# Causal attention on one NeuronCore: the four-block tile of each head takes its remainder through a PSUM bank

## The chip, the cores and the metric

The kernel runs on one core of one Trainium2 chip. The metric is the device time of one execution in microseconds. Engines are called PE (TensorE), ACT (ScalarE), DVE (VectorE), POOL (GpSimd) and SP (SyncE, which here only issues DMAs).

## The reference, cut to what matters

The whole program is one decoder layer on x of shape (4, 1024, 512): causal self attention with a linear position bias, cross attention against a context with a mask, and a quantised feed forward, each followed by a layer norm. The change touches the self attention alone:

```
q, k, v = heads(x @ Wq + bq), heads(x @ Wk + bk), heads(x @ Wv + bv)   # 16 heads of 32
scores = einsum('bhqd,bhkd->bhqk', q, k) / sqrt(32) + bias[None]
attn = softmax(scores, axis=-1)
out = einsum('bhqk,bhkd->bhqd', attn, v)
```

The bias is `slope * (k - q)` where allowed and -1e9 elsewhere. Even heads may look back (k <= q), odd heads forward (k >= q). There are 4 x 16 = 64 head instances of 1024 x 1024 scores, of which a little over half count.

## The kernel before

`attention_phase` is one function for both attentions; with `causal=True` it names its tiles `self_...`, without it `cross_...`. It holds one program for each engine, and the programs run loosely against each other through counting semaphores. Every engine carries out its own list strictly in order, so an instruction that waits holds up all that is behind it on that engine.

Work is cut into units `u`, 8 to a head and 32 to a loop pass (four heads, `HB`); `steps` runs first a prologue and then, for each step `t`, one call of `step(i, t, last)` on each engine. A head is worked twice over:

- **Row maxima** (`scores` L893 on PE, `maxima` L1128 on DVE). PE multiplies one block of 128 queries by all allowed keys into a score tile `sc[u % 2]` (two buffers). DVE adds the bias and takes the maximum of each row (L1147), which frees the buffer through the semaphore `taken`. Blocks come in the order big, small, big, small: widths 1024, 128, 896, 256, 768, 384, 640, 512. PE is 19 steps ahead with this (`SLEAD`).
- **Turning the maxima** (`turn_max` L907 on PE, `max_row` on ACT): once in a head the maxima are transposed through one of the `stp` banks and sent back by DMA as an extra row of the queries, so that the maximum is subtracted inside the next product.
- **Transposed scores** (`key_scores` L921 on PE, `exps` L1021 on ACT), 6 steps ahead (`ELEAD`). PE multiplies one block of 128 keys by all allowed queries (L939, with the triangle of the diagonal block added by L942), in chunks of at most 512 columns, into the two banks `stp[0]` and `stp[1]` in turn. ACT takes the exponential of each chunk in float32 into `p32` (L1033) and counts it in `expd`. PE may write chunk number c when chunk c-2 has been counted.
- **The remainder** (`low`, POOL L1239). The probability is used as two 16-bit parts: the upper half of the float32 word, read in place as bfloat16, and the remainder, p minus that upper half, which POOL writes as float16 into `plo`. In the self attention POOL does this for all eight tiles of a head; in the cross attention DVE does one in eight (L1161).
- **Values** (`values` L948 on PE). For each block of 128 queries PE adds upper part times values (L968) and remainder times values (L969) into the two output banks `ob`. It waits for `expd` and for POOL's count `lo_g`. The first tile of a head also waits for `o_read`, which says that the output banks of the head before have been read.
- **Finishing a head**: ACT copies half of the output banks (`oraw`, L1088), DVE adds the other half (`gather`, L1170, raising `o_read`), and two steps later DVE takes the reciprocal and writes the scaled result (`scale`, L1176 and L1183).

The order of a step on PE is: row scores of unit t+19, the turned maxima, transposed scores of unit t+6, values of unit t. On DVE it is: gather (when unit t is the first of a head), maxima of unit t+19, a remainder where DVE has one, scale. On ACT it is: exponentials of unit t+6, and the copies after the last unit of a head. Within a head the key blocks are taken in the widths 1024, 128, 896, 256, 768, 384, 640, 512, so the eighth unit of each head is the four-block tile of 512 columns: one chunk. Tiles of more than 512 columns are two chunks, so a head has 12 chunks. `p32` and `plo` hold eight units each. The PSUM banks are all in use: 4 for `sc`, 2 for `stp`, 2 for `ob`.

Row scores of an even numbered unit are at least 640 columns wide and use `sc[0]`; those of an odd numbered unit are at most 512 wide and use `sc[1]`.

Of the kernel before, what the change touches and what calls it, by code (L numbers as in the profile page):

```python
# [17 lines left out]
BF16 = mybir.dt.bfloat16  # L18
# [9 lines left out]
P = 128  # L28
# [543 lines left out]
def attention_phase(nc, c, name, causal, q_dram, k_dram, v_dram, out_dram, mb_dram=None, nm_dram=None, place_dram=None, kept=None, spare=None):  # L572
# [13 lines left out]
    with ExitStack() as ctx:  # L586
# [16 lines left out]
        osum = [sb(f"osum{j}", [P, ST, HD], F32) for j in range(2)]  # L603
        rden = [sb(f"rden{j}", [P, ST], F32) for j in range(2)]
        ost = sb("ost", [P, ST, HB * HD], F32)
        sc = [kit.ps(f"{name}_sc{j}", [P, S]) for j in range(2)]
        stp = [kit.ps(f"{name}_st{j}", [P, GT]) for j in range(2)]
        ob = [kit.ps(f"{name}_o{j}", [P, ST // 2, VW]) for j in range(2)]

# [5 lines left out]
        chunked = sem("chunked")  # L615
        expd = sem("expd")
        lo_v, lo_g = sem("lo_v"), sem("lo_g")
        pv_done = sem("pv_done")
        o_read = sem("o_read")
        o_recip, o_half, o_scaled = sem("o_recip"), sem("o_half"), sem("o_scaled")  # L620
# [85 lines left out]

        def on_vector(u):

            return not causal and u % UH == 4

        def width(u):

# [8 lines left out]
        def high_of(u):  # L721

            j, b = spot(u)
            return p32[j][:, b:b + width(u)].bitcast(BF16).rearrange("p (q h) -> p q h", h=2)[:, :, 1]

        def lows_of(u):
# [20 lines left out]
        with nc.Block() as block:  # L747
# [138 lines left out]
            @block.tensor  # L886
            def _(pe):
                def scores(i, u):

                    n, at, qt = rows_of(u)  # L890
                    j, slot = n % NQK, u
                    if at == 0:
                        pe.wait_ge(qk_in[j], (i + n // NQK + 1) * QKS)  # L893
                    pe.wait_ge(taken, i * (HB * UH) + slot + 1)
                    if not causal:
                        nc.tensor.matmul(sc[slot % 2][:, 0:GT], qa[j][0:HD, qt * P:(qt + 1) * P], ka[j][0:HD, 0:GT], start=True, stop=True)  # L896
                        nc.tensor.matmul(sc[slot % 2][:, GT:S], qa[j][HD:2 * HD, qt * P:(qt + 1) * P], kx[j][HD:2 * HD, :],  # L897
                                         start=True, stop=True).then_inc(scored, 1)
                        return
                    k0, k1 = key_range(n, qt)  # L900
                    for k in range(k0, k1, GT):
                        w = min(GT, k1 - k)
                        mm = nc.tensor.matmul(sc[slot % 2][:, k - k0:k - k0 + w], qa[j][0:3 * HD, qt * P:(qt + 1) * P],  # L903
                                              ka[j][0:3 * HD, k:k + w], start=True, stop=True)
                    mm.then_inc(scored, 1)

                def turn_max(i, n, cc, last=False):  # L907

                    pe.wait_ge(taken, i * (HB * UH) + (min(n + 1, HB) if last else n + 1) * UH + 2)
                    pe.wait_ge(expd, i * CS + cc + 1)  # L910
                    nc.tensor.transpose(stp[cc % 2][0:ST, 0:P], qmax[n % 2][:], c["idf"][:]).then_inc(chunked, 1)

                def ahead(i, u, last):
                    if within(last, u):
                        scores(i, u)

                def late_max(i, u, last):
                    if u % UH == TURN and within(last, u):
                        turn_max(i, u // UH + 1, turn_before(u), last)

                def key_scores(i, u):  # L921

                    n, at, kt = keys_of(u)
                    j = n % NQK
                    if at == 0:
                        pe.wait_ge(mrow_in[j], (i + n // NQK + 1) * 16)
                        if causal:
                            pe.wait_ge(place_in[j], (i + n // NQK + 1) * 16)
                    if at == 0 and isinstance(i, int) and i == 0:
                        pe.wait_ge(ready if n < 2 else ready_late, n % 2 + 1)  # L930
                    if not causal and n % HB == 0:
                        pe.wait_ge(nm_in[kt], (i + n // HB) // (H // HB) * 16 + 16)
                    cc = chunks_before(u)
                    for q0, q1 in chunks(n, kt):
                        pe.wait_ge(expd, i * CS + cc + 1)
                        w, out = q1 - q0, stp[cc % 2]
                        lhs = ka[j][0:KR, kt * P:(kt + 1) * P]
                        diag = causal and q0 <= kt * P < q1
                        mm = nc.tensor.matmul(out[:, 0:w], lhs, qa[j][0:KR, q0:q1], start=True, stop=causal)  # L939
                        if diag:  # L940
                            d = kt * P - q0
                            mm = nc.tensor.matmul(out[:, d:d + P], c["idbig"][:], tri[n % 2][:], start=False, stop=True, skip_group_check=True)  # L942
                        if not causal:
                            mm = nc.tensor.matmul(out[:, 0:w], c["idbig"][:], nm[kt][:, q0:q1], start=False, stop=True)  # L944
                        mm.then_inc(chunked, 1)
                        cc += 1

                def values(i, u):  # L948

                    n, at, kt = keys_of(u)  # L950
                    if at == 0:
                        pe.wait_ge(v_in[n % NQK], i * 16 + 16)
                        pe.wait_ge(o_read, (i * HB + n) * 2 + 2)
                    pe.wait_ge(expd, i * CS + chunks_by(u) + 2)
                    if on_vector(u):
                        pe.wait_ge(lo_v, i * LV + lows_by(u, True))
                    else:
                        pe.wait_ge(lo_g, i * LG + lows_by(u, False))
                    a, z = query_range(n, kt)
                    j, b = spot(u)  # L960
                    high, rest = high_of(u), plo[j][:, b:b + width(u)]
                    for qt in range(a // P, z // P):
                        q = slice(qt * P - a, qt * P - a + P)
                        out = ob[qt // 4]
                        first = at == 0 and qt % 4 == 0
                        last_kt = at == max(keys_of(n * UH + k)[1] for k in range(UH)
                                            if query_range(n, keys_of(n * UH + k)[2])[0] <= qt * P < query_range(n, keys_of(n * UH + k)[2])[1])
                        nc.tensor.matmul(out[:, qt % 4, :], high[:, q], vh[n % NQK][:, kt, :], start=first, stop=False, skip_group_check=True)  # L968
                        mm = nc.tensor.matmul(out[:, qt % 4, 0:HD + 1], rest[:, q], vh[n % NQK][:, kt, 0:HD + 1],  # L969
                                              start=False, stop=last_kt, skip_group_check=True)  # L970
                    mm.then_inc(pv_done, 1)
                    return mm

                def prologue():
                    for u in range(SLEAD):
                        ahead(0, u, False)
                        if u == UH + 1:
                            turn_max(0, 0, 0)
                        k = u - (SLEAD - ELEAD)
                        if k == 0 and causal:  # L980
                            pe.wait_ge(tri_made, 2)
                        if k >= 0:
                            late_max(0, k, False)
                            key_scores(0, k)

                def step(i, t, last):
                    ahead(i, t + SLEAD, last)
                    late_max(i, t + ELEAD, last)
                    if within(last, t + ELEAD):
                        key_scores(i, t + ELEAD)  # L990
                    values(i, t)

                steps(pe, prologue, step)
# [3 lines left out]
            def _(act):  # L997
# [23 lines left out]
                def exps(i, u):  # L1021
# [8 lines left out]
                    for q0, q1 in chunks(n, kt):  # L1030
                        act.wait_ge(chunked, i * CS + cc + 1)
                        bias = strip[n % NQK][:, S + kt:S + kt + 1] if causal else 0.0
                        nc.scalar.activation(p32[j][:, b + q0 - a:b + q1 - a], stp[cc % 2][:, 0:q1 - q0], ACT.Exp,  # L1033
                                             bias=bias, scale=SM).then_inc(expd, 1)
                        cc += 1
# [62 lines left out]
            def _(dve):  # L1098
# [55 lines left out]
                def low(i, u):  # L1154
                    n, at, kt = keys_of(u)
                    if not on_vector(u):
                        return
                    dve.wait_ge(expd, i * CS + chunks_by(u) + 2)
                    j, b = spot(u)
                    q = slice(b, b + width(u))  # L1160
                    nc.vector.tensor_tensor(plo[j][:, q], p32[j][:, q], high_of(u), ALU.subtract).then_inc(lo_v, 1)  # L1161

                def gather(i, n):

# [1068 lines left out]
```

## Time and profile before

| | |
|---|---|
| median of 3 runs | 3087.35 us (3085.69 to 3087.98) |
| profiled execution | 3089.86 us |
| its span, first to last instruction | 3088.1 us |
| mean granted TensorE clock | 0.936 |
| busy: PE, DVE, ACT, POOL | 85%, 73%, 61%, 59% |

The profile shows one execution. The self attention lies between about 370 and 975 us of its span, the cross attention between about 1138 and 2065 us. "Busy" is the time in which an engine had an instruction running; "idle before" is the gap in front of an instruction, with what ended it. PE's matmuls overlap, so their ends are modelled. On ACT, DVE and POOL the records of neighbouring instructions overlap slightly as well: by about 0.1 us on ACT and DVE and 0.04 us on POOL.

### The profile page before, as it was taken

To read this page: it belongs to the slowest core of one execution; us is meant where nothing else is said; L and a number is where in the kernel's file an instruction comes from. 1 tells how busy PE (TensorE), PEld (TensorE's weight loads), DVE (VectorE), ACT (ScalarE), POOL (GpSimd) and SP (SyncE) were. 2 spreads that over 40 slices of the span, in tenths; PEclk is the share of its full clock that TensorE was granted. 3 is DMA by queue.
4 is the path that set the end of the run, shared out by engine and by line. 5 is a ranking of instruction groups with operands and counts; after the bars stand their busy time and mean duration, and the time that the engine had idled before them with its cause. 6 is when DMAs were issued, how large, how long until landed. Compare 5 with 4: busy or idle time off the path is not lost. (4 is left out here: it accounts for less than half of the span.)

```text
span 3088.1 us, 77009 instructions
## 1 busy us (share of the span) xinstructions
PE 2625.1 (85%) x24103; PEld 1413.4 (46%) x24103; DVE 2253.0 (73%) x4459; ACT 1879.7 (61%) x3779; POOL 1808.1 (59%) x1209
## 2 busy tenths in 40 slices
PE   7999688888886869999999999962999899603999
PEld 4555245555554535555555555531444344301444
DVE  8888667777774777888888887847334477697776
ACT  3444377777775537777777777764333577695333
POOL 3444489999996319999999999986000244300000
PEclk9999789999998979999999999985999999856999
DMA  8999634444445661232131132135444688796332
GB/s 308 336 332 325 210 95 137 125 136 133 134 128 185 232 218 33 58 98 55 45 103 52 48 100 54 46 97 182 172 165 164 207 272 286 263 417 260 124 114 82
DMA packets 320616, 504.41 MB, mean 163 GB/s; under 512 B 36641, under 2 KB 158369, under 8 KB 320498
## 3 DMA queue, kind: packets, MB, share of 16 engines
q1 hardware_dynamic: 317026, 496.27, 48.3%
q0 software_dynamic: 1952, 6.29, 0.6%
q8 instruction: 55, 0.90, 0.1%
q10 hardware_dynamic: 1520, 0.43, 0.1%
q14 instruction: 63, 0.52, 0.1%
HBM read 266.10 MB, written 194.28 MB: 149 GB/s over the span
## 5 line engine op out<-in xcount | busy, mean ns | idle before, releaser
L1239 POOL TENSOR_TENSOR cross_plo<-cross_p 128x2048 f16<-128x2048 f32 (+1 forms) x256 | 850.4, 3350 | 77.2 <-ACT cross_p L1033 77.2
L1147 DVE CUSTOM_DVE_ANT_0 cross_junk<-cross_sc,rows 128x1024 bf16<-128x1024 f32 x512 | 622.7, 1223 | 149.3 <-PE cross_sc L897 146.3
L1033 ACT ACTIVATE cross_p<-cross_st 128x512 f32<-128x512 f32 x1024 | 556.3, 595 | 206.8 <-PE cross_st L944 206.8
L1239 POOL TENSOR_TENSOR self_plo<-self_p 128x1024 f16<-128x1024 f32 (+7 forms) x512 | 576.9, 1161 | 17.3 <-ACT self_p L1033 16.8
L1033 ACT ACTIVATE self_p<-self_st,self_strip 128x512 f32<-128x512 f32 (+3 forms) x768 | 415.6, 582 | 142.7 <-PE self_st L942 112.1
L1147 DVE CUSTOM_DVE_ANT_0 self_junk<-self_sc,self_strip 128x1024 bf16<-128x1024 f32 (+7 forms) x512 | 371.3, 752 | 135.2 <-PE self_sc L903 135.0
L939 PE MATMUL cross_st<-cross_qa,cross_ka 97*128 97x512 f16 x1024 | 396.0, 387 | 1.8 <-ACT cross_p L1033 0.7
L944 PE MATMUL cross_st<-rows,idbig 128*128 128x512 f16 x1024 | 391.6, 382 | 0.0
L968 PEld LDWEIGHTS cross_o<-cross_vh,cross_p 128*128 128x128 bf16 x4096 | 270.2, 97 | 76.2 <-issue 21.8
L968 PE MATMUL cross_o<-cross_vh,cross_p 128*128 128x65 f16 x4096 | 297.6, 191 | 4.9 <-POOL cross_plo L1239 4.5
L1851 POOL TENSOR_SCALAR v_w<-v_w 128x512 f32<-128x512 f32 x96 | 59.4, 618 | 401.9 <-ACT v_w L1828 401.9
L969 PE MATMUL cross_o<-cross_vh,cross_plo 128*128 128x33 f16 x4096 | 291.2, 179 | 0.0
L939 PE MATMUL self_st<-self_qa,self_ka 98*128 98x512 f16 (+3 forms) x768 | 246.7, 337 | 48.8 <-ACT self_p L1033 44.6
L969 PEld LDWEIGHTS cross_o<-cross_vh,cross_plo 128*128 128x128 f16 x4096 | 249.3, 96 | 53.4
L903 PE MATMUL self_sc<-self_ka,self_qa 96*128 96x512 f16 (+3 forms) x768 | 214.4, 336 | 34.0 <-DMA self_ka<-scr_k_hi 18.7
L968 PE MATMUL self_o<-self_vh,self_p 128*128 128x65 f16 x2304 | 200.1, 192 | 39.7 <-DVE self_osum L1170 19.8
L130 PE MATMUL gt_acc<-rows,wg_hi 128*128 128x512 f16 x768 | 230.5, 382 | 1.5 <-DVE rows L124 1.5
L896 PE MATMUL cross_sc<-cross_ka,cross_qa 32*128 32x512 f16 x512 | 200.6, 392 | 18.4 <-DMA cross_kx<-scr_k_hi 11.7
L897 PE MATMUL cross_sc<-cross_kx,cross_qa 32*128 32x512 f16 x512 | 200.6, 392 | 0.0
L968 PEld LDWEIGHTS self_o<-self_vh,self_p 128*128 128x128 bf16 x2304 | 164.0, 98 | 74.5 <-issue 44.2
L969 PE MATMUL self_o<-self_vh,self_plo 128*128 128x33 f16 x2304 | 192.5, 179 | 0.0
L939 PEld LDWEIGHTS cross_st<-cross_qa,cross_ka 97*128 97x128 f16 x1024 | 99.8, 97 | 187.8 <-ACT cross_p L1033 94.8
(263 smaller groups left out, 5845.6 us busy)
## 6 DMA issues: line engine op xcount, KB each, us to landing
self_strip<-self_strips SPq DMA_DIRECT2D x64, 516.0 KB, 3.2
scr_gate<-gt_y SPq DMA_DIRECT2D x96, 256.0 KB, 2.1
v_w<-scr_gate SPq DMA_DIRECT2D x96, 256.0 KB, 4.0
scr_h<-v_w SPq DMA_DIRECT2D x96, 256.0 KB, 4.1
j_h<-scr_h SPq DMA_DIRECT2D x48, 512.0 KB, 9.5
d_o<-scr_o SPq DMA_DIRECT2D x9, 1536.0 KB
scr_up<-v_y SPq DMA_DIRECT2D x48, 256.0 KB, 4.2
j_u<-scr_up SPq DMA_DIRECT2D x24, 512.0 KB, 12.1
```

What stands on the lines that cost most here:

```text
L130: mm = nc.tensor.matmul(out, a, b, start=(n == 0), stop=(n == len(terms) - 1))
L896: nc.tensor.matmul(sc[slot % 2][:, 0:GT], qa[j][0:HD, qt * P:(qt + 1) * P], ka[j][0:HD, 0:GT], start=True, stop=True)
L897: nc.tensor.matmul(sc[slot % 2][:, GT:S], qa[j][HD:2 * HD, qt * P:(qt + 1) * P], kx[j][HD:2 * HD, :], start=True, stop=True).then_inc(scor ...
L903: mm = nc.tensor.matmul(sc[slot % 2][:, k - k0:k - k0 + w], qa[j][0:3 * HD, qt * P:(qt + 1) * P], ka[j][0:3 * HD, k:k + w], start=True, st ...
L939: mm = nc.tensor.matmul(out[:, 0:w], lhs, qa[j][0:KR, q0:q1], start=True, stop=causal)
L944: mm = nc.tensor.matmul(out[:, 0:w], c["idbig"][:], nm[kt][:, q0:q1], start=False, stop=True)
L968: nc.tensor.matmul(out[:, qt % 4, :], high[:, q], vh[n % NQK][:, kt, :], start=first, stop=False, skip_group_check=True)
L969: mm = nc.tensor.matmul(out[:, qt % 4, 0:HD + 1], rest[:, q], vh[n % NQK][:, kt, 0:HD + 1], start=False, stop=last_kt, skip_group_check=True)
L1033: nc.scalar.activation(p32[j][:, b + q0 - a:b + q1 - a], stp[cc % 2][:, 0:q1 - q0], ACT.Exp, bias=bias, scale=SM).then_inc(expd, 1)
L1147: nc.vector.tensor_tensor_reduce(junk[slot % 2][:, 0:w], sc[slot % 2][:, 0:w], bias, 1.0, -3e38, ALU.add, ALU.max, qmax[n % 2][:, qt:qt + ...
L1239: nc.gpsimd.tensor_tensor(plo[j][:, a:z], p32[j][:, a:z], high, ALU.subtract).then_inc(lo_g, 1)
L1851: nc.gpsimd.tensor_scalar(wk[n % NW][:], wk[n % NW][:], 65536.0, MAGIC, ALU.mult, ALU.add).then_inc(inc, 1)
```

## The change

The four-block tile of each causal head, the eighth unit, is taken off POOL:

- `sc[1]` shrinks from two banks to one, and the bank that comes free becomes `whole`.
- PE writes the tile's transposed scores to `whole` instead of `stp[cc % 2]`. It first waits until DVE has finished with `whole` for the head before (`lo_v`).
- ACT takes the exponential twice: once rounded to bfloat16 into `p32` (semaphore `high_made`), once in float32 from `whole` back into `whole`; only the second counts in `expd`.
- DVE subtracts the bfloat16 values from `whole` and writes `plo`, in the step in which it does the maxima of the unit with 512 columns, after these. `values` waits for `high_made`, `expd` and `lo_v`.
- POOL has seven tiles left in a head. All other tiles, and the cross attention, are as they were.

```
-        sc = [kit.ps(f"{name}_sc{j}", [P, S]) for j in range(2)]
+        sc = [kit.ps(f"{name}_sc{j}", [P, GT if causal and j else S]) for j in range(2)]
...
+        if causal:
+            whole, high_made = kit.ps(f"{name}_whole", [P, GT]), sem("high_made")
...
         def on_vector(u):
 
-            return not causal and u % UH == 4
+            return u % UH == (UH - 1 if causal else 4)
...
         def high_of(u):
 
             j, b = spot(u)
+            if causal and on_vector(u):
+                return p32[j][:, b:b + width(u) // 2].bitcast(BF16)
             return p32[j][:, b:b + width(u)].bitcast(BF16).rearrange("p (q h) -> p q h", h=2)[:, :, 1]
...
                     cc = chunks_before(u)
+                    if causal and on_vector(u) and (not isinstance(i, int) or i > 0 or u >= UH):
+                        pe.wait_ge(lo_v, i * LV + lows_by(u, True) - 1)
                     for q0, q1 in chunks(n, kt):
                         pe.wait_ge(expd, i * CS + cc + 1)
-                        w, out = q1 - q0, stp[cc % 2]
+                        w, out = q1 - q0, whole if causal and on_vector(u) else stp[cc % 2]
...
                     pe.wait_ge(expd, i * CS + chunks_by(u) + 2)
+                    if causal and on_vector(u):
+                        pe.wait_ge(high_made, i * LV + lows_by(u, True))
...
                         bias = strip[n % NQK][:, S + kt:S + kt + 1] if causal else 0.0
+                        if causal and on_vector(u):
+                            nc.scalar.activation(high_of(u), whole[:], ACT.Exp, bias=bias, scale=SM).then_inc(high_made, 1)
+                            nc.scalar.activation(whole[:], whole[:], ACT.Exp, bias=bias, scale=SM).then_inc(expd, 1)
+                            continue
...
+                    if causal:
+                        dve.wait_ge(high_made, i * LV + lows_by(u, True))
                     dve.wait_ge(expd, i * CS + chunks_by(u) + 2)
...
-                    nc.vector.tensor_tensor(plo[j][:, q], p32[j][:, q], high_of(u), ALU.subtract).then_inc(lo_v, 1)
+                    nc.vector.tensor_tensor(plo[j][:, q], whole[:] if causal else p32[j][:, q], high_of(u), ALU.subtract).then_inc(lo_v, 1)
```

## Rows read from the trace of the kernel before

**Rows 1.** The page: span, and POOL's busy tenths in 40 slices of 77 us.

```profile
span 3088.1 us, 77009 instructions
...
POOL 3444489999996319999999999986000244300000
```

**Rows 2.** One stretch: busy us of PE, PEld, DVE, ACT, POOL; clock, DMA.

```profile
440.00:680.00 240.00, 202.14 (x2809) 127.63 (x2809) 183.49 (x535) 183.19 (x400) 239.58 (x213) 1.00 0.43 133
```

**Rows 3.** The line L1239 between 440 and 960 us, and who waited for it.

```profile
L1239 POOL TENSOR_TENSOR self_plo<-self_p x462: 392/1144/2077, 439.9 to 959.7; 128x512 f16<-128x512 f32 x20, 128x896 f16<-128x896 f32 x20, 128x384 f16<-128x384 f32 x19, 128x1024 f16<-128x1024 f32 x19
...
who waited for it (us, times):
busy tenths in 40 slices 0000039999994000000000000000000000000000
```

**Rows 4.** ACT's timeline around 701 us: start, length, instruction, idle before.

```profile
700.61 0.69 ACT L1033 ACTIVATE self_p<-self_st,self_strip 128x512 f32<-128x512 f32 x1 [1.09 <-PE self_st L942]
...
701.78 0.69 ACT L1033 ACTIVATE self_p<-self_st,self_strip 128x512 f32<-128x512 f32 x1
...
707.25 0.43 ACT L1088 COPY self_oraw<-self_o 128x132 f32<-128x132 f32 x2
```

**Rows 5.** POOL's timeline at 702.6 us: the 1024-column tile.

```profile
702.56 2.08 POOL L1239 TENSOR_TENSOR self_plo<-self_p 128x1024 f16<-128x1024 f32 x1
```

**Rows 6.** DVE's timeline from 700 to 710 us.

```profile
702.28 0.60 DVE L1183 TENSOR_TENSOR self_ost<-self_osum,self_rden 128x256 f32<-128x256 f32 x1 [0.21 <-DVE self_rden L1176]
702.81 0.81 DVE L1147 CUSTOM_DVE_ANT_0 self_junk<-self_sc,self_strip 128x640 bf16<-128x640 f32 x1
...
704.67 1.23 DVE L1147 CUSTOM_DVE_ANT_0 self_junk<-self_sc,self_strip 128x1024 bf16<-128x1024 f32 x1 [0.43 <-PE self_sc L903]
...
706.73 1.09 DVE L1147 CUSTOM_DVE_ANT_0 self_junk<-self_sc,self_strip 128x896 bf16<-128x896 f32 x1 [0.62 <-PE self_sc L903]
...
707.75 0.48 DVE L1170 TENSOR_TENSOR self_osum<-self_o,self_oraw 128x128 f32<-128x128 f32 x2
```

**Rows 7.** PE's timeline from 701 to 709 us.

```profile
701.35 0.39 PE L939 MATMUL self_st<-self_qa,self_ka 98*128 98x512 f16 x1 [0.29 <-ACT self_p L1033]
...
701.97 0.43 PE L903 MATMUL self_sc<-self_ka,self_qa 96*128 96x512 f16 x2
...
703.51 0.18 PE L969 MATMUL self_o<-self_vh,self_plo 128*128 128x33 f16 x1
703.68 0.60 PE L903 MATMUL self_sc<-self_ka,self_qa 96*128 96x512 f16 x2
...
705.96 0.55 PE L903 MATMUL self_sc<-self_ka,self_qa 96*128 96x512 f16 x2
...
708.36 0.20 PE L968 MATMUL self_o<-self_vh,self_p 128*128 128x65 f16 x1 [0.56 <-DVE self_osum L1170]
```

**Rows 8.** POOL's tiles by shape, 440 to 960 us: busy, mean ns, idle before.

```profile
L1239 POOL TENSOR_TENSOR self_plo<-self_p 128x1024 f16<-128x1024 f32 x58 | 118.9, 2050 | 0.5 <-ACT self_p L1033 0.2
L1239 POOL TENSOR_TENSOR self_plo<-self_p 128x896 f16<-128x896 f32 x58 | 97.2, 1675 | 0.0
...
L1239 POOL TENSOR_TENSOR self_plo<-self_p 128x512 f16<-128x512 f32 x58 | 60.1, 1037 | 0.0
```

**Rows 9.** ACT by shape, 440 to 960 us.

```profile
L1033 ACT ACTIVATE self_p<-self_st,self_strip 128x512 f32<-128x512 f32 x347 | 229.0, 688 | 76.2 <-PE self_st L942 60.1 <-PE self_st L939 14.0 <-PE self_o L969 2.1
```

**Rows 10.** DVE by shape, 440 to 960 us.

```profile
L1183 DVE TENSOR_TENSOR self_ost<-self_osum,self_rden 128x256 f32<-128x256 f32 x58 | 40.6, 700 | 8.2 <-DVE self_rden L1176 3.0
L1147 DVE CUSTOM_DVE_ANT_0 self_junk<-self_sc,self_strip 128x512 bf16<-128x512 f32 x58 | 39.4, 680 | 0.0
...
L1170 DVE TENSOR_TENSOR self_osum<-self_o,self_oraw 128x128 f32<-128x128 f32 x116 | 28.0, 283 | 2.9 <-ACT self_oraw L1088 2.9
```

**Rows 11.** DVE's remainder in the cross attention, 1160 to 2060 us: ns min/median/max.

```profile
L1161 DVE TENSOR_TENSOR cross_plo<-cross_p x64: 1219/1220/3481, 1170.6 to 2053.9; 128x1024 f16<-128x1024 f32 x64
```

## The prediction

> **What bounds the kernel now.** I read the page first, then the busy times of a stretch, then who waits for whom, then the timelines of single engines through one head.
>
> The page puts the self attention in slices 5 to 12, where POOL's digit is 9 [rows 1]. In a stretch of 240 us POOL is busy for 239.58, PE for 202.14, DVE for 183.49, ACT for 183.19, at full clock [rows 2]. So at first sight POOL sets the pace, and the change takes an eighth of its instructions away. That reading has to be checked, because an engine can be full without anyone waiting for it.
>
> The check is who waited for POOL's line between 440 and 960 us: the list is empty, for 462 tiles [rows 3]. The only consumer of a remainder is `values` on PE. In the head that I follow, the 1024-column tile runs on POOL from 702.56 to 704.64 [rows 5] and PE starts on its values at 708.36, 3.7 us later, released by DVE's `osum` [rows 7]. On the other side POOL starts that tile 0.1 us after ACT has ended the second of its two chunks at 701.78 + 0.69 = 702.47 [rows 4, 5]. POOL is fed just in time and is never late. Its own need is below the period: the 512-column tile takes 1.037 us and the 896-column tile 1.675, so 0.213 for each further 128 columns, and the 1024-column tile should take 1.89, but takes 2.05 [rows 8]. POOL fills the head because that tile is stretched, not because others queue for it.
>
> What then makes a head 9.02 us long (462 tiles, eight to a head, start from 439.9 to 959.7: 519.8 / 461 x 8) [rows 3]? I walk the chain round once.
> - DVE ends `osum` at 707.75 + 0.48 = 708.23, PE starts `values` of the first tile at 708.36 [rows 6, 7]. One head earlier this was about 699.34.
> - Behind it on PE stand the 768-column row scores and the special tile's transposed scores. ACT had waited 1.09 us for these when it starts at 700.61 [rows 4].
> - PE's second chunk of the 1024 tile waits for ACT's count of the special tile, ended at about 701.30, and starts at 701.35 [rows 7]. It stands in front of `values`, and these in front of the 640-column row scores, which run from 701.97 to 702.40.
> - DVE takes the 640 maximum at 702.81 [rows 6]. Handing row scores from PE to DVE costs 0.22 us (705.96 + 0.55 = 706.51 to 706.73), so it could have begun at 702.62: PE is 0.19 early here, and DVE came out of the scaling, L1183, only then.
> - It ends at 702.81 + 0.81 = 703.62 and frees the buffer; PE writes the 1024-column row scores at 703.68. PE's own last matmul before that started at 703.51; the slack of PE's queue there is at most 0.1 us.
> - DVE waited 0.43 us for them, starts at 704.67, ends at 705.90; PE writes the 896-column scores at 705.96; DVE waited 0.62, starts at 706.73, ends at 707.82 and does `osum` [rows 6, 7].
>
> So the loop runs PE, ACT (the special tile alone), PE, DVE, PE, DVE, and back. POOL is not in it, except that it may hold DVE up in L1183.
>
> **The change, part by part.**
>
> *POOL gets one tile less.* 1.037 us a head, 66 us over 64 heads [rows 8], off an engine for which nobody waits: worth nothing by itself. Through L1183 it can be worth something. That instruction has 256 columns and takes 700 ns, more than a maximum over 512 columns at 680 [rows 10]; the special tile runs on POOL just then (it ends at 702.6, as the next one starts). Without it L1183 would end earlier, but the 640 maximum could only move up by PE's 0.19 us: a gain of at most 0.19 a head, 12 us in all, if nothing else came later. The Trainium skill, "SBUF — State Buffer", section "Who interferes with whom", says that a DVE instruction with two SBUF inputs contends with GpSimd's reads and one with at most one does not; L1183 has two, and the trace agrees. By that page alone the sum would be a gain of up to 12 us.
>
> *ACT gets a second exponential of 512 columns.* It lies exactly where the loop passes through ACT. The mean of such an instruction is 688 ns [rows 9], but back to back they follow each other every (701.78 - 700.61) / 2 = 0.585 us, with two pitches between those starts [rows 4]. The second instruction is the one that counts in `expd`, so the second chunk of the 1024 tile starts 0.59 us later. The 1.09 us in which ACT is idle is no cover: it ends when the special tile's scores arrive, before the first of the two. The trace has no exponential that writes PSUM; bounds are 0.69 (no overlap) and 0.49: two copies of 132 columns take 0.43, so 0.22 for one [rows 4], the columns beyond these cost (0.585 - 0.22) / 380 = 0.96 ns each, and 512 at that price with nothing fixed are 0.49. I take 0.59, the row of the same size. The Trainium skill, "ScalarE: Activation LUTs", section "Step-by-step: what each stage is for", has PSUM as the lower-latency destination of ScalarE; no row here shows it. By it the sum would be nearer to the low bound.
>
> PE is in order, so `values` and the 640-column row scores come 0.59 late. At the 640 maximum 0.19 of this is slack: DVE is 0.40 late. At the 1024-column row scores PE's own queue decides: its 0.59 less at most 0.10 leaves 0.49 or more, against 0.40 through DVE. From there to `osum` and back to PE the loop has no slack, so a head becomes 0.49 to 0.59 longer. The new bank doesn't help PE to run ahead: its waits are counted in chunks as before.
>
> *DVE gets the subtraction.* 512 columns with one input in PSUM: nearest are the 512-column maximum at 680 ns with PSUM and SBUF inputs, and half of the cross attention's 1220, which is 610 [rows 10, 11]. I take 0.65 and bounds of 0.55 and 0.75. It stands between the 512 maximum and the 1024 maximum, where DVE now idles 0.43 us [rows 6]. DVE is 0.40 late there and the scores of the 1024 tile about 0.50 late, so the gap is 0.43 + 0.10 = 0.53; the subtraction needs 0.65 and sticks out by 0.12 (0.02 to 0.22). Its inputs have been ready since about 702, and its consumer, `values` of the special tile, comes some 2 us later. The `osum` instructions, also PSUM with SBUF, hold 283 ns beside a POOL that never rests [rows 10], so I expect no stretch.
>
> *Waits.* PE waits once more before the special tile's scores, on a subtraction done half a head earlier, and once more before its values; DVE waits on two counts long reached. In front of the special tile the extra wait is on the loop, but behind matmuls that are still running. I take 0.02 us a head, between 0 and 0.05.
>
> *ACT's later work.* It is shifted by the same 0.59 and catches up in small gaps; the copies at 707.25 [rows 4] were ready about 0.15 before DVE wanted them and shift no more than DVE does. Nothing is added.
>
> *Sum.* 0.50 + 0.12 + 0.02 = 0.64 a head if DVE's overhang and PE's queue add up in full; where PE's slack and the low end of the subtraction hold, 0.50 + 0.02. I take 0.57. The first heads, before 440 us, run the same lists more slowly and pay about the same. In the last two heads, where no row scores are left, POOL runs behind, and a tile less gives back a microsecond or two. 62 heads at 0.57 are 35, less 1: 34 us. On the profiled span, 3088.1 becomes 3122, its execution 3089.9 becomes 3124; on the median of 3087.35, 3122.
>
> Bounds: the low ones throughout (0.49 - 0.10 + 0.02 = 0.41 a head) give 62 x 0.41 - 1 = 24 us, 3112; the high ones (0.69 + 0.22 + 0.05 = 0.96) give 59, 3146, but they hardly come together; 0.80 a head gives 3136.
>
> **The rivals.**
>
> *A. POOL does set the pace (faster).* If the empty list of waits misleads and DVE and PE only follow POOL, a head shrinks until the next engine is full. POOL would need 8.0 us a head, DVE 183.49 / 240 x 9.02 + 0.65 = 7.5, ACT 6.9 + 0.6 = 7.5, PE 7.6. The head could fall by up to 1.0, in practice by about 0.5: 3087 - 62 x 0.5 = 3056, at the outside 3025. A weaker form is the 0.19 of L1183 with the second exponential somehow off the loop: 3075. For it speaks the full POOL [rows 2]; against it, that no one waits for it, with 3.7 us to spare. It decides from the point at which `values` starts right behind POOL's tile. Chance 0.09.
>
> *B. It is a wash.* The second exponential is absorbed, because PE's and DVE's slack is larger than the records let me see (PE's ends are modelled), and freed L1183 time gives back the rest: within 6 us of 3087. Chance 0.07.
>
> *C. The subtraction is stretched (slower).* The cross attention's version has a maximum of 3481 ns beside a minimum of 1219 [rows 11]. If POOL's 1024 tile, 1.9 us, blocks DVE's new instruction, a head grows by 1 us or more beyond the forecast: 3122 + 62 = 3184 or more. `osum` and the maxima speak against it. Chance 0.04.
>
> **How the numbers follow.** The forecast has 0.80; most of it lies between 3106 and 3140. The range goes from 3096 to 3144, a little past its bounds, since a mechanism that I follow through four engines may be a tenth or two of a microsecond off a head; it leaves out A, B and C. About 0.2%, or 6 us, is what a measurement of this kernel can tell from no change. Faster: A, 0.09. Same: B, 0.07. Slower: the forecast and C, 0.84.
>
> **What the profile after would show.** ACT's special tile as two 512-column instructions 0.59 apart behind one idle of about 1 us; the second chunk of the 1024 tile on PE at about 0.6 later within the head; a head of about 9.6 us; POOL idle for over 1.5 us of each, before the 1024 tile; DVE's idle before the 1024 maximum gone or nearly so; L1183 nearer to its shortest, with idle behind it. The prediction is wrong if heads get shorter, or if DVE's new instruction is far from 0.65 us.

## The result, and the profile after

| | before | after |
|---|---|---|
| median | 3087.66 us (4 runs, 3085.69 to 3092.61) | 3153.86 us (4 runs, 3146.30 to 3171.28) |
| ratio | | 1.021, 95% interval 1.0179 to 1.0240 |
| span of the profiled execution | 3088.1 us | 3169.5 us |
| self attention, first to last instruction | 365.1 to 975.4 us | 365.5 to 1038.1 us |

The change costs 66 us; I had forecast 34, with 3144 as the upper end. The direction and the place are right, the size is half. The profiled execution is the slowest of the four: of its 81 us, 62 lie in the self attention (672.6 us against 610.3), and 19 in the norm behind the cross attention. There a single small DVE instruction (L1571, 2 columns) takes 22.7 us, where the longest of its 16 takes 0.8 us in the profile before. Of the other kept profiles only the one with the subtraction cut has such an instruction, of 11.7 us. Its cause is open; the change doesn't touch it.

The page first: span, POOL and the granted clock in 40 slices.

```profile
span 3169.5 us, 77158 instructions
...
POOL 3444477787787325999999999984200144400000
PEclk9999789999998797999999999985899999956999
```

POOL's digits of 8 and 9 in the self attention are now 7 and 8, as expected. The clock has 9, 8 and 7 through the self attention. The stretches say it more clearly (busy us of PE, PEld, DVE, ACT, POOL, then clock and DMA):

```profile
440.00:680.00 240.00, 191.20 (x2545) 120.13 (x2543) 175.72 (x508) 180.26 (x388) 190.60 (x169) 0.94 0.38 120
680.00:920.00 240.00, 190.73 (x2535) 120.54 (x2533) 175.15 (x505) 179.05 (x387) 190.67 (x171) 0.94 0.38 119
```

Against [rows 2] POOL falls from 239.58 to 190.60, and the granted clock from 1.00 to 0.94. That last number is what my forecast has no term for. Next, DVE's timeline over two heads; a head is the distance between two `osum` rows.

```profile
741.25 0.48 DVE L1184 TENSOR_TENSOR self_osum<-self_o,self_oraw 128x128 f32<-128x128 f32 x2
...
744.71 0.43 DVE L1197 TENSOR_TENSOR self_ost<-self_osum,self_rden 128x256 f32<-128x256 f32 x1
746.39 0.82 DVE L1159 CUSTOM_DVE_ANT_0 self_junk<-self_sc,self_strip 128x640 bf16<-128x640 f32 x1 [1.26 <-PE self_sc L907]
...
747.82 0.69 DVE L1175 TENSOR_TENSOR self_plo<-self_whole,self_p 128x512 f16<-128x512 f32 x1
748.99 1.22 DVE L1159 CUSTOM_DVE_ANT_0 self_junk<-self_sc,self_strip 128x1024 bf16<-128x1024 f32 x1 [0.49 <-PE self_sc L907]
...
752.07 0.48 DVE L1184 TENSOR_TENSOR self_osum<-self_o,self_oraw 128x128 f32<-128x128 f32 x2
...
755.54 0.42 DVE L1197 TENSOR_TENSOR self_ost<-self_osum,self_rden 128x256 f32<-128x256 f32 x1
756.51 0.82 DVE L1159 CUSTOM_DVE_ANT_0 self_junk<-self_sc,self_strip 128x640 bf16<-128x640 f32 x1 [0.55 <-PE self_sc L907]
...
757.87 0.69 DVE L1175 TENSOR_TENSOR self_plo<-self_whole,self_p 128x512 f16<-128x512 f32 x1
758.48 1.22 DVE L1159 CUSTOM_DVE_ANT_0 self_junk<-self_sc,self_strip 128x1024 bf16<-128x1024 f32 x1
...
761.54 0.48 DVE L1184 TENSOR_TENSOR self_osum<-self_o,self_oraw 128x128 f32<-128x128 f32 x2
```

The first head takes 752.07 - 741.25 = 10.82 us, the second 9.47. The second is the head that I forecast: 9.02 + 0.57 = 9.59. What sets the first apart is the clock (stretches of that time):

```profile
740.00:744.40 4.40, 2.73 (x39) 1.53 (x36) 3.22 (x11) 3.04 (x8) 4.04 (x5) 1.00 0.47 156
744.50:747.90 3.40, 3.40 (x34) 2.13 (x35) 2.01 (x7) 1.97 (x4) 2.04 (x2) 0.50 0.31 99
747.90:751.00 3.10, 2.83 (x44) 1.91 (x42) 2.05 (x6) 2.38 (x6) 2.49 (x4) 1.00 0.00 1
```

From 744.5 to 747.9 the clock is at 0.50, the 1.2 GHz level, and PE is busy for all of it. DVE waits 1.26 us for the 640-column scores instead of 0.55, and 0.49 for the 1024-column ones instead of nothing. The fall comes just behind PE's longest wait of the head (the second row below, 0.89 us):

```profile
743.14 0.38 PE L945 MATMUL self_st<-self_qa,self_ka 98*128 98x512 f16 x1
744.41 0.54 PE L945 MATMUL self_st<-self_qa,self_ka 98*128 98x512 f16 x1 [0.89 <-ACT self_whole L1043]
```

Before, the same wait was 0.29 us [rows 7]. In the whole stretch it is much the same: of the 16 low stretches between 430 and 950 us, 14 begin within 0.3 us of the end of this wait, before or behind it, and the other two 1.4 and 2.2 us behind the wait of 0.5 to 0.6 us that PE has in front of `values`. But the wait is in every head and the clock falls in one of three; what picks the head is not shown.

On ACT the two exponentials, in the full-clock head, and the next one:

```profile
753.95 0.69 ACT L1042 ACTIVATE self_p<-self_whole,self_strip 128x512 bf16<-128x512 f32 x1 [1.10 <-PE self_whole L948]
754.54 0.65 ACT L1043 ACTIVATE self_whole<-self_whole,self_strip 128x512 f32<-128x512 f32 x1
755.11 1.71 ACT L1045 ACTIVATE self_p<-self_st,self_strip 128x512 f32<-128x512 f32 x3
```

And DVE by shape, 440 to 960 us, for comparison with [rows 10]:

```profile
L1175 DVE TENSOR_TENSOR self_plo<-self_whole,self_p 128x512 f16<-128x512 f32 x52 | 35.7, 686 | 0.0
...
L1197 DVE TENSOR_TENSOR self_ost<-self_osum,self_rden 128x256 f32<-128x256 f32 x52 | 22.1, 425 | 7.6 <-DVE self_rden L1190 2.8
```

I counted 53 of the 64 heads in this way, the sixth to the fifty-eighth (462 to 991 us here). 36 run wholly at full clock and take 9.50 us on the mean, 0.49 more than the 9.02 before. 17 touch a low stretch and take 10.97. Between 430 and 950 us the clock is low for 64.8 us in all; before, there was no low stretch there.

### The profile page after: what moved, and what is told of

The parts are those of the page before. It is cut to its first block and busy times, and to the rows that moved or that the text cites. A ratio compares the mean times of both kernels' runs of the same rounds, so it can differ in the third digit from the quotient of the medians.

```text
span 3169.5 us, 77158 instructions
## 1 busy us (share of the span) xinstructions
PE 2656.1 (84%) x24103; PEld 1434.0 (45%) x24103; DVE 2295.9 (72%) x4523; ACT 1916.2 (60%) x3843; POOL 1737.6 (55%) x1145
## 5 line engine op out<-in xcount | busy, mean ns | idle before, releaser
L1253 POOL TENSOR_TENSOR self_plo<-self_p 128x1024 f16<-128x1024 f32 (+6 forms) x448 | 506.5, 1162 | 148.3 <-ACT self_p L1045 147.8
L1045 ACT ACTIVATE self_p<-self_st,self_strip 128x512 f32<-128x512 f32 (+3 forms) x704 | 378.4, 573 | 98.5 <-PE self_st L948 66.3
L945 PE MATMUL self_st<-self_qa,self_ka 98*128 98x512 f16 (+3 forms) x704 | 236.9, 358 | 82.2 <-ACT self_whole L1043 54.2
L907 PE MATMUL self_sc<-self_ka,self_qa 96*128 96x512 f16 (+3 forms) x768 | 226.0, 352 | 35.7 <-DMA self_ka<-scr_k_hi 18.7
L976 PE MATMUL self_o<-self_vh,self_p 128*128 128x65 f16 x2304 | 212.1, 197 | 39.3 <-DVE self_osum L1184 19.8
L976 PEld LDWEIGHTS self_o<-self_vh,self_p 128*128 128x128 bf16 x2304 | 176.3, 104 | 78.5 <-issue 47.3
L977 PE MATMUL self_o<-self_vh,self_plo 128*128 128x33 f16 x2304 | 202.2, 185 | 0.0
```

What stands on the lines that cost most here:

```text
L1253: nc.gpsimd.tensor_tensor(plo[j][:, a:z], p32[j][:, a:z], high, ALU.subtract).then_inc(lo_g, 1)
```

## The experiments

Theory 1: the second exponential lengthens the loop by about 0.5 us a head, and PE's longer wait behind it makes the clock fall in some heads, which costs the other half. Theory 2: the second half is DVE's subtraction, or something about the lent PSUM bank. Each comparison is with the kernel before; "head" is the mean of the heads at full clock, "touched" the number of the same 53 heads that a low stretch touches; both come from the one profiled execution of each kernel. The row "before" has the lowest and the highest of the medians that the kernel before had beside these kernels.

| kernel | median us | ratio, 95% interval | head us | touched | clock 440 to 920 us |
|---|---|---|---|---|---|
| before | 3087.2 to 3088.5 | | 9.02 | 0 | 1.00 |
| after | 3153.9 | 1.0210 (1.0179 to 1.0240) | 9.50 | 17 | 0.94 |
| second exponential alone | 3145.9 | 1.0203 (1.0182 to 1.0223) | 9.45 | 16 | 0.93 |
| ... of 256 columns | 3108.3 | 1.0072 (1.0054 to 1.0090) | 9.24 | 4 | 0.98 |
| after, work for PE in the long wait | 3115.8 | 1.0094 (1.0078 to 1.0111) | 9.52 | 0 | 1.00 |
| after, work for PE elsewhere | 3149.4 | 1.0188 (1.0148 to 1.0229) | 9.50 | 19 | 0.94 |
| after, subtraction cut | 3146.8 | 1.0188 (1.0171 to 1.0205) | 9.43 | 18 | 0.93 |
| DVE from SBUF, one exponential | 3118.2 | 1.0112 (1.0092 to 1.0133) | 9.30 | 10 | 0.96 |
| after, one wait less on PE | 3097.4 | 1.0034 (1.0022 to 1.0047) | 9.22 | 0 | 1.00 |
| after, first exponential counts | 3100.2 | 1.0032 (1.0014 to 1.0050) | 9.22 | 0 | 1.00 |
| one wait less, subtraction cut | 3098.4 | 1.0029 (1.0014 to 1.0045) | 9.22 | 0 | 1.00 |
| one wait less, earlier scaling | 3099.9 | 1.0032 (1.0020 to 1.0045) | 9.21 | 0 | 1.00 |
| before, POOL's tile cut | 3080.3 | 0.9982 (0.9965 to 0.9999) | 8.88 | 0 | 1.00 |
| before, earlier scaling | 3088.5 | 1.0002 (0.9992 to 1.0012) | 9.00 | 0 | 1.00 |

**The second exponential alone.** To the kernel before:

```
+                        if causal and u % UH == UH - 1:
+                            nc.scalar.activation(again[:], stp[cc % 2][:, 0:q1 - q0], ACT.Exp, bias=bias, scale=SM)
                         nc.scalar.activation(p32[j][:, b + q0 - a:b + q1 - a], stp[cc % 2][:, 0:q1 - q0], ACT.Exp,
                                              bias=bias, scale=SM).then_inc(expd, 1)
```

> The kernel before, with one thing added: ACT takes a second exponential of the four-block tile, 512 columns into a bfloat16 tile that nobody reads, ahead of the one that counts. POOL still makes the remainder, DVE gets nothing. Theory 1 (the second exponential lies in the loop of a head, and PE's longer wait behind it makes the granted clock fall in some heads): heads of 9.5 to 9.6 us at full clock, some at 10.7 or more with a granted clock under 1.00 between 440 and 920 us, 3140 to 3165 us in all. Theory 2 (what goes beyond my 34 us is DVE's subtraction or the lent PSUM bank): full clock, 3087 + 32 = about 3119 us.

It gives 3145.9 us: 58.7 of the 66 us, with no subtraction on DVE, no lent bank, and POOL doing all eight tiles. As the source of the second half theory 2 is out. The full-clock head is 0.43 us longer than before.

**Work for PE in the long wait.** To the kernel after, with the output banks declared whole and the unread columns zeroed once at the start:

```
+                        if causal and u % UH == 0 and cc == chunks_before(u) + 1:
+                            for _ in range(6):
+                                nc.tensor.matmul(obank[0][:, 264:GT], ka[j][0:KR, 0:P], qa[j][0:KR, 0:GT - 264], start=False, stop=True, skip_group_check=True)
                         pe.wait_ge(expd, i * CS + cc + 1)
```

> The changed kernel, and six matmuls of 248 columns in front of PE's wait for the counted exponential, once a head, into columns of an output bank that nobody reads: about 0.6 us of work on PE inside a wait of 0.9 us. Theory 1: the loop stays as long as in the changed kernel at full clock (9.5 us a head), but the clock no longer falls: granted clock 1.00 between 440 and 920 us, 3115 to 3125 us. If the clock has another cause, or the slow heads do, nothing changes or it gets slower: 3146 to 3171 us.

PE's timeline of this kernel at the place of the wait:

```profile
743.39 0.38 PE L950 MATMUL self_st<-self_qa,self_ka 98*128 98x512 f16 x1
743.61 0.80 PE L945 MATMUL self_o<-self_qa,self_ka 98*128 98x248 f16 x6
...
744.67 0.39 PE L950 MATMUL self_st<-self_qa,self_ka 98*128 98x512 f16 x1 [0.26 <-ACT self_whole L1050]
```

The wait of 0.89 is down to 0.26 and the head is as long as before the filling, 9.52. The stretch from 440 to 920 us:

```profile
440.00:920.00 480.00, 407.63 (x5605) 267.26 (x5604) 364.29 (x1058) 373.81 (x807) 396.65 (x353) 1.00 0.40 125
```

Full clock, and 3115.8 us: useless work on PE takes 38 us off the changed kernel. What is left, 28.6 us, is the loss without the clock: 0.45 a head over all 64 heads.

**The same kind of work elsewhere.** Four such matmuls in front of the first chunk of the 768-column tile, where PE waits less; the long wait stays.

```
+                        if causal and u % UH == 4 and cc == chunks_before(u):
+                            for _ in range(4):
+                                nc.tensor.matmul(obank[0][:, 264:GT], ...)
```

> The changed kernel with four of the unread matmuls at another place of the head: in front of the first chunk of the 768-column tile, where PE waits 0.2 to 0.5 us for ACT, and not in the long wait behind the four-block tile. If the clock falls because of that one long wait: granted clock 0.94 between 440 and 920 us as in the changed kernel, 3146 to 3171 us. If it falls because PE has too little to do over a head as a whole, wherever the gap is: clock 0.98 or more, 3115 to 3135 us.

```profile
744.11 0.39 PE L950 MATMUL self_st<-self_qa,self_ka 98*128 98x512 f16 x1 [0.89 <-ACT self_whole L1050]
```

The row is PE's wait, unchanged; the clock is 0.94 and the time 3149.4. PE does have more to do (393.69 us busy between 440 and 920 us, against 381.93 in the changed kernel), so adding some work to the head is not enough. It was four matmuls here and six there, and neither six at this place nor four in the long wait was run: that the place decides, and not the amount, is likely but not shown.

**A shorter second exponential.** The kernel with the second exponential alone, cut to 256 columns.

```
-                            nc.scalar.activation(again[:], stp[cc % 2][:, 0:q1 - q0], ACT.Exp, bias=bias, scale=SM)
+                            nc.scalar.activation(again[:, 0:256], stp[cc % 2][:, 0:256], ACT.Exp, bias=bias, scale=SM)
```

> The kernel before with an added exponential of 256 columns at the four-block tile instead of 512, into a tile that nobody reads. Its pitch should be about 0.36 us (0.96 ns less for each of 256 columns). Theory 1, with a clock that falls only when PE's work in a head gets too sparse: heads of 9.3 us at full clock, 3087 + 64 x 0.27 = about 3105 us if the clock stays at 1.00, 3110 to 3125 us if it already falls in some heads. If the clock fell through the extra instruction as such and not through PE's wait, it would fall as often as with 512 columns.

Heads of 9.24 us (0.23 more than before, where I had 0.27), and 4 touched heads instead of 16. The instruction as such does not bring the clock down as often as with 512 columns; PE's wait behind it is about 0.7 us here and 0.9 there. Together with the filled wait this points at the wait, not at the instruction.

**The subtraction cut to 128 columns.** To the kernel after, with the other columns of `plo` zeroed once:

```
-                    nc.vector.tensor_tensor(plo[j][:, q], whole[:] if causal else p32[j][:, q], high_of(u), ALU.subtract).then_inc(lo_v, 1)
+                    if causal:
+                        nc.vector.tensor_tensor(plo[j][:, b:b + P], whole[:, 0:P], high_of(u)[:, 0:P], ALU.subtract).then_inc(lo_v, 1)
+                        return
+                    nc.vector.tensor_tensor(plo[j][:, q], p32[j][:, q], high_of(u), ALU.subtract).then_inc(lo_v, 1)
```

> The changed kernel, with DVE's subtraction cut to the first 128 columns; the remainder of the other 384 is left at zero, so the output lacks them. It measures the term of my sum for the subtraction, 0.12 us a head. If the subtraction sticks out: full-clock heads of 9.4 instead of 9.5 and 5 to 8 us less, the clock falling as before, 3138 to 3165 us. If it lies wholly in DVE's idle time: no difference, 3146 to 3171 us. If it were a main cause of what I missed: 30 us less, about 3120 us.

The head falls from 9.50 to 9.43: the subtraction sticks out by 0.07 us, where I had 0.12. The median is 7 us lower, within what the changed kernel's own runs spread over.

**DVE from SBUF with one exponential.** To the kernel before, one line; `low` on DVE then serves the self attention too:

```
-            return not causal and u % UH == 4
+            return u % UH == (UH - 1 if causal else 4)
```

> The kernel before, with the remainder of the four-block tile made by DVE from the float32 probabilities in SBUF (two SBUF inputs) instead of by POOL; ACT takes one exponential as before and no PSUM bank is lent. The second exponential is gone, so theory 1 has PE's wait as short as before and the clock at 1.00; DVE's 0.69 us against a gap of 0.43 gives up to 0.26 us a head, less up to 0.19 from the freed scaling: 3085 to 3105 us. If the subtraction on DVE were what cost 64 us, this would be as slow as the changed kernel, near 3150; if it is blocked by POOL's 1024 tile (up to 1.9 us) it would be slower still.

A miss of mine, 3118.2 for 3085 to 3105. DVE and POOL by shape, 440 to 960 us:

```profile
L1161 DVE TENSOR_TENSOR self_plo<-self_p 128x512 f16<-128x512 f32 x55 | 54.9, 999 | 0.0
...
L1239 POOL TENSOR_TENSOR self_plo<-self_p 128x128 f16<-128x128 f32 x55 | 46.6, 847 | 0.0
```

The subtraction with both inputs in SBUF takes 999 ns, with one in PSUM 686; POOL's 128-column tile, which runs just then, takes 847 instead of the 394 that it takes before. The clock is at 0.96 here too, with ten touched heads, though ACT has no second exponential: PE's waits for DVE's maxima grew to 24.6 us in all between 440 and 920 us, from 0.2 before. So the clock isn't bound to that one wait on ACT; another added wait can bring it down. It need not fall right behind the added wait: all ten low stretches of the counted heads begin within 0.5 us behind PE's wait of 0.56 to 0.67 us in front of `values`, which the kernel before has too [rows 7], and 2.4 to 2.8 us behind the new wait of about 0.5 us. The longer head (9.30) and the ten touched heads (10.31 on the mean) together make up most of the 31 us.

**One wait less on PE.** In the changed kernel PE still counts chunks as if the four-block tile used one of the two `stp` banks. It doesn't, so the second chunk of the 1024 tile may be written as soon as the first.

```
-                        pe.wait_ge(expd, i * CS + cc + 1)
+                        if not (causal and on_vector(u - 1 if u else UH - 1) and u % UH == 0 and (not isinstance(i, int) or i > 0 or u >= UH) and cc > chunks_before(u)):
+                            pe.wait_ge(expd, i * CS + cc + 1)
```

> The changed kernel, but PE no longer waits for ACT's counted exponential before the second chunk of the 1024 tile: with the four-block tile in its own bank, that chunk's bank was last used two chunks earlier, which the wait of the first chunk already covers. If the loop is lengthened only through this one wait: 9.0 us a head, full clock, 3085 to 3095 us. If ACT's list itself is nearly full, so that the 0.59 us comes back at the next handovers (the first tile of 128 columns waits for the 1024 tile's first chunk, the next for its second): 9.3 to 9.5 us a head, but PE's stall is split up and the clock stays higher: 3105 to 3130 us. If the wait didn't matter at all: 3146 to 3171 us.

3097.4 us, 56 us under the changed kernel, and between my two forecasts: the head is 9.22, where I had 9.0 or 9.3 to 9.5. PE's timeline: both chunks at once, and the wait has moved to the next tile and shrunk to 0.53.

```profile
705.92 0.38 PE L946 MATMUL self_st<-self_qa,self_ka 98*128 98x512 f16 x1
706.14 0.22 PE L949 MATMUL self_st<-self_tri,idbig 128*128 128x128 f16 x1
706.20 0.38 PE L946 MATMUL self_st<-self_qa,self_ka 98*128 98x512 f16 x1
...
707.80 0.23 PE L946 MATMUL self_st<-self_qa,self_ka 98*128 98x128 f16 x1 [0.53 <-ACT self_p L1046]
```

ACT's timeline shows that it now runs from the four-block tile through the 1024 tile and the 128-column one without a gap:

```profile
705.90 0.69 ACT L1043 ACTIVATE self_p<-self_whole,self_strip 128x512 bf16<-128x512 f32 x1 [1.09 <-PE self_whole L949]
706.49 0.66 ACT L1044 ACTIVATE self_whole<-self_whole,self_strip 128x512 f32<-128x512 f32 x1
707.06 1.53 ACT L1046 ACTIVATE self_p<-self_st,self_strip 128x512 f32<-128x512 f32 x3
```

**The first exponential counts.** To the kernel after, with the two counts exchanged; SP's reload of the strip waits for one chunk more.

```
-    ... activation(high_of(u), whole[:], ...).then_inc(high_made, 1)
-    ... activation(whole[:], whole[:], ...).then_inc(expd, 1)
+    ... activation(high_of(u), whole[:], ...).then_inc(expd, 1)
+    ... activation(whole[:], whole[:], ...).then_inc(high_made, 1)
```

> The changed kernel with the two counts of the four-block tile exchanged: the first exponential (bfloat16) counts in expd, the second in high_made; the strip's reload on SP waits for one chunk more. PE's second chunk of the 1024 tile starts at the same point of a head as in the kernel before. Same question as for the kernel without that wait, asked in another way: 9.0 us a head and full clock if only the wait matters (3085 to 3095), 9.3 to 9.5 if ACT's own list carries the delay on (3105 to 3130).

The same head of 9.22 and 3100.2 us, by another way. Which semaphore the second exponential raises was worth some 54 us.

**What is left of the loss there.** The kernel with one wait less, and the subtraction cut as above:

> The changed kernel without PE's wait before the second chunk of the 1024 tile, and with DVE's subtraction cut to 128 columns (the remainder of the other 384 columns is left at zero). It tells what is left of the loss there, 9.22 us a head against 9.02. If it is DVE's list: a head of 9.0, about 3087 us. If it is ACT's second exponential at the later handovers: 9.2 us a head, 3094 to 3101 us.

The head stays at 9.22 us: the rest is not DVE's. That it is ACT's fuller list, at the later handovers, fits the gapless rows above; I did not take the second exponential out of that kernel.

**POOL's tile cut.** To the kernel before, with those columns of `plo` zeroed once:

```
                     j, a, z = lows_of(u)
+                    if causal and u % UH == UH - 1:
+                        z = a + P
```

> The kernel before, but POOL makes the remainder of the four-block tile for its first 128 columns only; the other 384 are left at zero, so the output lacks them. POOL is freed of 0.64 us a head and nothing is added elsewhere. If POOL sets the pace: 64 x 0.64 = 41 us less, about 3046. If POOL is outside the loop and only holds up DVE's scaling L1183: at most 0.19 us a head, 3075 to 3087 us, with POOL idle in each head.

POOL is freed of 0.64 us a head and the head gets 0.14 shorter, 7 us in all; if POOL set the pace it would have been 41. The 0.14 goes with a shorter L1183, by shape:

```profile
L1183 DVE TENSOR_TENSOR self_ost<-self_osum,self_rden 128x256 f32<-128x256 f32 x59 | 25.7, 435 | 8.3 <-DVE self_rden L1176 3.0
```

435 ns instead of 700 [rows 10].

**Earlier scaling.** To the kernel before, and to the one with one wait less:

```
-                    n = to_finish(i, t, SCALE if causal else 0)
+                    n = to_finish(i, t, 0)
```

> The kernel before, with DVE's scaling of a finished head (L1176, L1183) moved up by two steps, from behind the 384-column maximum to behind the 256-column one, where DVE idles 0.95 us. If L1183, held up by POOL, stands in the loop of a head as I read it in the trace: up to 0.14 us a head, as in the kernel whose POOL had less to do, so 3079 to 3084 us. If POOL, needing 8.85 us of a head of 9.02 without stretches, is the next limit, the gain ends near 3 us. If the scaling only moves its collision with POOL to another tile: no change.

> The changed kernel without PE's wait for the counted exponential before the second chunk of the 1024 tile, and with the scaling two steps earlier. If the rest of that kernel's loss (9.22 us a head against 9.02) lies in ACT's fuller list: no change from it, 3094 to 3101 us. If it lies in DVE's list, which now has the subtraction: the 0.9 us of scaling leave the stretch between the 768 and the 640 maximum and a head gets shorter, 3080 to 3092 us.

Neither moves. In the first, DVE's and POOL's rows by shape say why:

```profile
L1183 DVE TENSOR_TENSOR self_ost<-self_osum,self_rden 128x256 f32<-128x256 f32 x58 | 73.7, 1271 | 8.2 <-DVE self_rden L1176 3.0
```

```profile
L1239 POOL TENSOR_TENSOR self_plo<-self_p 128x384 f16<-128x384 f32 x58 | 57.6, 993 | 0.0
```

The scaling now meets POOL's 384-column tile: it takes 1271 ns for 700, and the tile 993 for 822, while the 1024-column tile is back to 1888 from 2050. The collision has moved, and POOL stays full. Of the kernels that make the whole remainder, none beats the kernel before.

## Why the prediction was right and wrong

- **That POOL is full but outside the loop**: right. Three quarters of its tile taken away would have been 41 us on a pace set by it, and gave 7 (POOL's tile cut). That it enters through L1183: it fits, 0.14 us a head for my bound of 0.19, with L1183 at 435 ns for 700. Rival A is out.
- **The second exponential, 0.59 us in the loop**: right in place and nearly in size. From start to start it is 754.54 - 753.95 = 0.59 us for the first and 755.11 - 754.54 = 0.57 for the one that writes PSUM; in length they are 687 and 653 ns. Alone it made the full-clock head 9.45 - 9.02 = 0.43 us longer, where the sum has 0.50. The Trainium skill, "ScalarE: Activation LUTs", section "Step-by-step: what each stage is for", calls PSUM the lower-latency destination of ScalarE. The trace agrees in sign, with a gain of 0.02 us in pitch that matters little here.
- **The subtraction**: 686 ns for my 650; it sticks out by 0.07 for my 0.12. With one input in PSUM it takes 685 to 689 ns in all 52 heads, though POOL is at work on a tile for most of that time; with both in SBUF it takes 999 on the mean, and POOL's tile beside it 847 for 394. The Trainium skill, "SBUF — State Buffer", section "Who interferes with whom", says that DVE with two SBUF inputs contends with GpSimd's reads, and with at most one does not; both kernels agree. The two also read the bfloat16 values in different layouts, which no run separates. Rival C, the stretched subtraction, is out.
- **The sum of 0.57 a head**: measured 0.49 at full clock, and 28.6 us for the kernel whose clock was held up, for my 34 (which on the median of 3087.35 gives 3121, not the 3122 that I wrote). Up to here the working stands, and rival B, the wash, is out.
- **The step that failed** is one that isn't there: the sum has no term for the clock. I wrote "at full clock" of the stretch before and carried it over, while lengthening PE's wait from 0.29 to 0.89 us a head. The runs showed that this wait brings the granted clock of the stretch from 1.00 to 0.94, and with PE's wait filled it is 1.00 again. The lost clock costs 3153.9 - 3115.8 = 38 us by the medians, more than everything that I had priced. The self attention of the two profiled executions is 672.6 us against 638.0 with the filled wait, a difference of 34.6: 24 of it lie in the 53 counted heads (528.6 us against 504.8; 17 x (10.97 - 9.50) gives 25), and the other 11 before and behind them, where the clock is low for 46 us against 3. The rest of the 38 is within the spread of the changed kernel's four runs.
- **"The new bank doesn't help PE to run ahead: its waits are counted in chunks as before"**: right about the kernel as written, and I stopped there. The bank would have helped; with the count corrected the loss is 10 us instead of 66.
- **The bounds** covered the costs that I listed and not a state that the costs can bring about. 3144 as the upper end was 10 short.

## What to carry to other kernels

When a change lengthens a wait of TensorE, look at the granted clock of that stretch, and price the case in which it falls: here the fall cost more than the wait. A unit that is 100% busy is the bound only if someone waits for it. When a buffer is taken out of a rotation, go through the waits that count the rotation: one that was needed before the change and is needless after it cost 56 us here.

## What the runs showed of the hardware that I had not expected

- Six matmuls that nobody reads, in a wait of 0.89 us once in 9.5 us, brought the granted clock from 0.94 to 1.00 and the time from 3153.9 to 3115.8 us. Four in another wait of the head changed nothing (0.94, 3149.4).
- The kernels whose heads were 9.22 us or shorter kept the full clock, one of 9.24 had 4 touched heads of 53, one of 9.30 had 10, those of 9.43 to 9.50 had 16 to 19. The kernel with filled waits kept it at 9.52: it is not the length of the head. What exactly the chip looks at stays open.
- How often the clock fell can't be read from the spread of the times. The changed kernel's four runs lie between 3146.3 and 3171.3 us, but the four with work for PE elsewhere, with 19 touched heads, within 3.6 us, and twelve of the kernel before between 3082.97 and 3102.13. Each kernel has one profile, so whether the same heads are hit each time is open.
- DVE and POOL hold each other up when DVE has both inputs in SBUF: 999 ns against 686 for 512 columns on DVE, and 847 against 394 for the 128-column tile on POOL.
